# Two attention loops: three score banks in a ring, one bank for weighted sums, values products in halves

## What is computed

```python
x = _layernorm(x + _L0_attn_ref(x, ...))                      # recurrence and channel mix
x = _layernorm(x + _L0_xattn_ref(x, ctx_1024, mask, ...))     # attention 0
x = _layernorm(x + _L0_ffn_ref(x, ...))
x = _layernorm(x + _L1_attn_ref(x, ...))                      # linear recurrence
x = _layernorm(x + _L1_xattn_ref(ctx_1024, x, ...))           # attention 1
x = _layernorm(x + _L1_ffn_ref(x, ...))                       # 8 experts, 2 per position

def attention(x, ctx, ...):            # q from x (2048), k and v from ctx (1601 rows)
    scores = q @ k.T * scale           # per head, 2048 x 1601
    attn = softmax(scores)             # attention 0: masked keys at -inf
    return (attn @ v) @ Wo.T
```

## Time and profile before

| | |
|---|---|
| median of three runs | 2498.0 us |
| span of the profiled execution | 2495.9 us |
| PE busy | 1964.2 us (79% of the span) |
| DVE busy | 1159.1 us (46%) |
| ACT busy | 1035.0 us (41%) |
| mean granted TensorE clock | 0.917 of 2.4 GHz |
| narrow attention, first score product to last copy of weighted sums | 359.4 to 628.6 us |
| wide attention, the same | 1173.5 to 1959.5 us |

### The profile page before, as it was taken

The page is one execution under the profiler, slowest core; times in us unless marked ns, Lnnn a source line. Parts: engine busy times, 40 slices in busy tenths (PEclk is TensorE's granted clock), DMA queues, the critical chain, the costliest instruction groups (busy, mean ns, idle before and its releaser), DMA issues.

```text
span 2495.9 us, 27607 instructions
## 1 busy us (share of the span) xinstructions
PE 1964.2 (79%) x7552; PEld 794.0 (32%) x7553; DVE 1159.1 (46%) x1674; ACT 1035.0 (41%) x1606; POOL 221.1 (9%) x188
## 2 busy tenths in 40 slices
PE   5789869998798757628888888888887627999990
PEld 2334412222243223303222222222221225666660
DVE  4652367664211434438767667666660121111114
ACT  2332327666312343301666566666667501222220
POOL 1030100000201003200000000000000140000004
PEclk8899969999899879857999999999999958999995
DMA  7000130001000000370000000000000351000003
GB/s 252 0 0 0 33 94 25 25 21 53 1 0 4 0 0 27 69 127 7 8 7 14 8 8 7 8 15 8 7 1 1 140 207 33 28 26 28 27 26 103
DMA packets 63282, 90.41 MB, mean 36 GB/s; under 512 B 14144, under 2 KB 56320, under 8 KB 61514
## 3 DMA queue, kind: packets, MB, share of 16 engines
q1 hardware_dynamic: 60106, 80.77, 11.1%
q0 software_dynamic: 3072, 8.39, 1.1%
HBM read 61.53 MB, written 27.20 MB: 36 GB/s over the span
## 4 chain that ended last, share of the span: by engine, by line
PE 45%; issue 10%; ACT 9%; DVE 5%; POOL 2%; DMA 2%; ACTq 1%; SPq 1%; DVEq 0%; POOLq 0%
PE ps L1046 8%; PE ps L1652 8%; PE ps L512 8%; ACT arena L1119 7%; PE ps L1037 6%; PE ps L982 4%; PE ps L1667 4%; DVE arena L1149 2%; PE ps L1310 2%; DMA qparts<-arena 1%; PE ps L1076 1%; PE ps L440 1%; POOL arena L1766 1%; PE ps L1660 1%; PE ps L1065 1%
## 5 line engine op out<-in xcount | busy, mean ns | idle before, releaser
L1119 ACT ACTIVATE arena<-ps,arena 128x512 f32<-128x512 f32 x1088 | 668.0, 683 | 448.5 <-PE ps L1037 447.0
L1149 DVE TENSOR_REDUCE arena<-ps 128x1 f32<-128x832 f32 (+1 forms) x768 | 674.2, 908 | 213.5 <-PE ps L982 207.9
L1037 PE MATMUL ps<-arena 100*128 100x512 bf16 x1088 | 389.9, 389 | 119.4 <-ACT arena L1119 109.0
L512 PE MATMUL ps<-arena 128*128 x832 | 379.7, 616 | 83.0 <-DVE arena L1451 25.0
L982 PE MATMUL ps<-arena 97*128 97x416 bf16 (+1 forms) x1280 | 364.0, 367 | 90.8 <-DMA arena<-qparts 61.9
L1046 PE MATMUL ps<-arena 128*32 128x512 f32 x2160 | 289.3, 608 | 0.0
L1037 PEld LDWEIGHTS ps<-arena 100*128 100x128 bf16 x1088 | 93.9, 96 | 524.2 <-ACT arena L1119 443.2
L512 PEld LDWEIGHTS ps<-arena 128*128 128x128 f32 x832 | 162.7, 197 | 298.0 <-issue 298.0
L1652 PE MATMUL ps<-arena 128*128 x608 | 198.2, 469 | 29.4 <-ACT arena L1720 29.4
L982 PEld LDWEIGHTS ps<-arena 97*128 97x128 bf16 x1280 | 121.5, 99 | 246.9 <-DVE arena L1149 104.2
L1847 DVE TENSOR_TENSOR arena<-ps,arena 128x352 f32<-128x352 f32 x76 | 39.9, 525 | 272.5 <-ACT arena L1727 272.5
(11 more groups left out here) (186 smaller groups left out, 1403.7 us busy)
## 6 DMA issues: line engine op xcount, KB each, us to landing
arena<-in_experts_w SPq DMA_DIRECT2D x8, 2176.0 KB, 17.3
arena<-qparts SPq DMA_DIRECT2D x192, 64.0 KB, 2.3
qparts<-arena SPq DMA_DIRECT2D x24, 256.0 KB, 6.1
rows_in<-arena SPq DMA_DIRECT2D x1, 5120.0 KB, 31.8
arena<-kparts SPq DMA_DIRECT2D x12, 416.0 KB, 23.4
arena<-rows_in SPq DMA_DIRECT2D x38, 128.0 KB
rows_out<-arena SPq DMA_DIRECT2D x38, 128.0 KB, 1.7
arena<-in_w_rwkv SPq DMA_DIRECT2D x1, 2560.0 KB, 11.2
```

Of the source, the lines that this page charges most:

```text
L512: ins = eng.matmul(out, w[:, k, m * P:(m + 1) * P], x[:, k, tok(c)], start=k == 0, stop=k == ktiles - 1)
L1037: eng.matmul(score_bank(k), Kst[0:ROWS, g * HG + h, kt * P:(kt + 1) * P], Qst[0:ROWS, g, h, :], start=True, stop=True).then_inc(st_full.se ...
L1119: eng.activation(probs[:, keys_of(u, kt) % 2, h, :], score_bank(k), ACT.Exp, bias=zero_col).then_inc(p_full.sem, 1)
L1149: eng.tensor_reduce(MX[:, par, h * QT + q, e:e + 1], slot_banks(s_static)[:, 0:SIDE, 0:seg_keys], AX.XY, ALU.max).then_inc(slot_free.sem, 1)
```

## The change

All of it is in `attend` and what it calls.

1. **Ring of three score banks.** Banks 5, 6 and 7 take the scores in turn; score number k waits for the reader of number k-3. The denominators' product (`den`) no longer overwrites the old weighted sums but takes its own place in the ring.
2. **One bank for the weighted sums** (4). The first values product of a unit waits until the sums of the unit before are copied (`o_copied`). ScalarE makes this copy, no longer VectorE; it stands behind the fourth exponential of the next unit's first tile.
3. **Values products in halves.** Each is cut into two of 256 columns (`PV_CUTS`), placed at two points of the tile.
4. **New order in a tile**: score 0, item, score 1, score 2, first half of the values, item, score 3, second half, (third item). Wide: `den` stands between scores 1 and 2 of tile 2.
5. **First pass over 1602 keys** in the wide case: products over 401, 401, 400 and 400 keys (before: four of 416). In the narrow case an item is two heads, in the two banks of a slot, with one maximum that writes both, negated, in place; `negate` falls away there. 8 items per unit, two per tile.
6. The turn of the maxima waits for all maxima before it (`slot_free` up to s_count; before: s_count - 1).
7. Exponentials, logarithms and inversions take the bias as an immediate 0.0.

```diff
+            RING, RING_UNIT = 3, HG * n_kt + 1
+            PV_CUTS = 2
-            AT_DEN, AT_TURN, AT_INVERT, AT_OUT = (1, 1, 2, 3) if window else (2, 5, 4, 8)
+            AT_DEN, AT_TURN, AT_OUT = (1, 1, 3) if window else (2, 5, 8)
...
                 for kt in range(n_kt):
                     want = PAIRS * (kt + 1) // n_kt if first_pass else 0
-                    mid = (taken + want) // 2
+                    mine = list(range(taken, want)) + [None] * 3
+                    values = (kt - 1, 0) if kt else (n_kt - 1, -1)
                     yield ("scores", kt, 0)
-                    if kt == 0 and u > 0:
-                        yield ("pv", n_kt - 1, -1)
+                    if mine[0] is not None:
+                        yield ("item", mine[0])
                     yield ("scores", kt, 1)
-                    for pair in pairs[taken:mid]:
-                        yield ("pair",) + pair
+                    if kt == AT_DEN and u > 0 and not window:
+                        yield ("den",)
                     yield ("scores", kt, 2)
+                    if has_values:
+                        yield ("pv",) + values + (0,)
+                    if mine[1] is not None:
+                        yield ("item", mine[1])
                     yield ("scores", kt, 3)
...
+            def ring_bank(r):
+                return ps[:, 5 + r % RING, :]
+            def ring_wait(eng, u, i, r):
+                if r >= RING:
+                    ring_read.wait(eng, ring_before(i) + (r - RING + 1))
...
-            def score_bank(k):
-                return ps[:, 4 + k % 2, :]
-            def o_bank(u):
-                return ps[:, 6 + u % 2, :]
+            o_bank = ps[:, 4, :]
...
                 def turn_max(i_par, s_static, s_count):
-                    slot_free.wait(eng, s_count - 1)
+                    slot_free.wait(eng, s_count)
...
+                def values(w, kt, cut):
+                    at = cut * PVW
+                    for h in range(HG):
+                        ins = eng.matmul(o_bank[32 * h:32 * h + 32, at:at + PVW], Vaug[:, kt, (w % 4) * HG + h, :],
+                                         probs[:, keys_of(w, kt) % 2, h, at:at + PVW],
+                                         start=kt == 0 and cut == 0, stop=kt == n_kt - 1 and cut == PV_CUTS - 1,
...
+                            if kt == 0 and cut == 0 and u > 0:
+                                o_copied.wait(eng, i)
+                            values(u + before, kt, cut)
...
+                def copy_o(u, i):
+                    pv_done.wait(eng, n_kt * i)
+                    if u >= 3:
+                        o_norm.wait(eng, i - 2)
+                    eng.activation(Osb[:, (u - 1) % 2, :], o_bank, ACT.Copy).then_inc(o_copied.sem, 1)
...
-                            eng.activation(probs[:, keys_of(u, kt) % 2, h, :], score_bank(k), ACT.Exp,
-                                           bias=zero_col).then_inc(p_full.sem, 1)
+                            eng.activation(probs[:, keys_of(u, kt) % 2, h, :], ring_bank(r), ACT.Exp,
+                                           bias=0.0).then_inc(ring_read.sem, 1)
```

More of the change, by code:

```diff
@@ L870, in plan @@
                 first_pass = u <= 5
-                pairs = [(q, h, e) for q in range(QT) for h in range(HG) for e in range(ENDS)] if first_pass else []
                 taken = 0
@@ L895, in plan, with ring_place, ring_before, values_after @@
                         yield ("out", 1)
+            def ring_place(u, step):
+                return [s for s in plan(u) if s[0] in ("scores", "den")].index(step)
+            def ring_before(i):
+                return 0 if isinstance(i, int) and i == 0 else i * RING_UNIT - 1
+            def ring_bank(r):
[3 more added lines that the diff above has]
+                    ring_read.wait(eng, ring_before(i) + (r - RING + 1))
+                elif u > 0:
+                    lengths = {1: (RING_UNIT - 1, RING_UNIT)}.get(u, (RING_UNIT,))
+                    late = min((n - 1 - r) % RING for n in lengths)
+                    ring_read.wait(eng, ring_before(i) - late)
             BASE = 2 * PAIRS + 1
-            def values_after(i, q, h, e):
-                n = (q * HG + h) * ENDS + e
+            def values_after(i, n):
                 return range(n_kt * n // PAIRS, n_kt * (n + 1) // PAIRS) if i == 1 else ()
             def slots_before(u):
-                return BASE + sum(1 for v in range(u) for s in plan(v) if s[0] in ("pair", "turn_max", "out"))
+                return BASE + sum(1 for v in range(u) for s in plan(v) if s[0] in ("item", "turn_max", "out"))
             assert slots_before(5) - slots_before(1) == SLOTS
@@ new lines, in unit @@
+                            r = ring_place(u, step)
+                            ring_wait(eng, u, i, r)
+                            eng.matmul(ring_bank(r), Kst[0:ROWS, g * HG + h, kt * P:(kt + 1) * P],
+                                       Qst[0:ROWS, g, h, :], start=True, stop=True).then_inc(ring_full.sem, 1)
+                        elif what == "pv":
+                            _, kt, before, cut = step
+                            if before:
+                                ring_read.wait(eng, ring_before(i))
+                            else:
+                                ring_read.wait(eng, ring_before(i) + (ring_place(u, ("scores", kt, HG - 1)) + 1))
+                            if kt == 0 and cut == 0 and u > 0:
+                                o_copied.wait(eng, i)
+                            values(u + before, kt, cut)
+                        elif what == "item":
+                            _, n = step
@@ L1063, in unit @@
                         elif what == "den":
-                            o_copied.wait(eng, i)
-                            eng.matmul(o_bank(u - 1), pick_den, Osb[:, (u - 1) % 2, :], start=True,
-                                       stop=True).then_inc(den_out.sem, 1)
+                            denominators(u, i, ring_place(u, step))
                         elif what == "out":
@@ L1080, in _ @@
                 run_units(eng, unit)
-                p_full.wait(eng, 4 * n_kt * 16)
-                for h in range(HG):
-                    ins = eng.matmul(o_bank(15)[32 * h:32 * h + 32, :], Vaug[:, n_kt - 1, 3 * HG + h, :],
-                                     probs[:, keys_of(7, n_kt - 1) % 2, h, :], start=False, stop=True)
-                ins.then_inc(pv_done.sem, 1)
-                o_copied.wait(eng, 16)
-                eng.matmul(o_bank(15), pick_den, Osb[:, 1, :], start=True, stop=True).then_inc(den_out.sem, 1)
+                ring_read.wait(eng, ring_before(16))
+                for cut in range(PV_CUTS):
+                    values(7, n_kt - 1, cut)
+                denominators(8, 16, 0)
                 s = slots_before(8)
@@ L1111, in unit @@
                     i = unit_of(u, c)
+                    to_invert = None
                     for step in plan(u):
```

190 lines of the change are left out of this document (96 added, 94 removed).

## The result

Four runs of the changed kernel gave 2332.31 to 2334.47 us, median 2333.1, against 2498.08 for four runs of the kernel before: a ratio of 0.934, 95% interval 0.933 to 0.936. The forecast was 2334. The profiled span fell from 2495.9 to 2332.6 us, by 163.3.

What follows compares the result with a forecast made beforehand. TensorE was taken as the bound, losing time to mutual waits with ScalarE. Savings of 103 + 21 + 30 + 6 + 4 = 164 us from 2495.9 gave 2332, with 2.1 added 2334 us; range 2300 to 2400.

Steps and rivals of the forecast that it cites:

- The bound: Wide loops: TensorE, busy 536 of 608 us, is nearest to full; it and ScalarE each wait once per tile.
- The price of a half: Values product on TensorE: a half costs 0.66 us, 0.24 fixed plus 2 x 0.213; possible from 0.43 to 1.09.
- rival E: Values products: a half costs nearly a whole, 1.09 us, so the kernel gets slower, 2565 us; chance 0.06.
- Wide units with a first pass: Wide loops: a unit takes 41.0 us against 48.35, 7.3 saved in each of 14 units, 103 us.
- Rival D: Looped wide and narrow units: the denser TensorE stream runs out of instructions, +58 us, 2392 us; chance 0.08.
- The turn: Turn of the maxima in a wide unit: 0.11 us as before plus 0.45 for waiting for the item just ahead.
- Narrow units: Narrow loops: a unit with a first pass takes 13.7 us against 15.83, 30 us saved; last two units 6.
- First passes ahead of the loops: Stretches where VectorE sets the pace: 64 wide items x 0.03 us, about as much narrow, 4 us saved.
- B: Unit starts: the first values product waits for the copy of sums, 1.5 us in 32 units, 2382 us; chance 0.14.
- C: Each tile: one score wait of 0.28 us remains on TensorE, +67 us, 2401 us; chance 0.08.
- F: Whole change: nothing comes of it, TensorE's work fills what it gains at 0.9 us a half; chance 0.02.
- A: Whole kernel: the sum of savings holds, 2334 us, own range 2305 to 2365; chance 0.62.

## Why the prediction was right

- **The bound.** TensorE and ScalarE waited for each other, TensorE was the fuller one, and with the waits gone it is the bound: 88% busy before, 98% after. The run with two banks brings the waits back, and 110 us; the run over 1664 keys shows that more columns on TensorE are more time.
- **The price of a half** was 0.66 us, from rows 3 and 5: measured 0.66. This was the widest term, between 0.43 and 1.09, and the one on which rival E hung; the run with the halves together shows that the fixed part belongs to the visit to the 32-column form. Beside this price the prediction puts the time without a drain 65 us lower, 0.12 us for each of 544 halves. That is the price of doubling the visits; without any fixed part its own 0.24 a half would make 131.
- **Wide units with a first pass**: 41.0 us worked out, 41.25 measured; 14 units were to give 103. First to last copy and the first unit gave 118.2, the last two units 23.1 of it (21 expected), 95 for the others. Some 8 us are missing: 0.25 a unit, and the units with a Wo product, of which the three saved 6.3, 3.9 and 7.1 us instead of 7.3 (51.8, 53.8 and 48.1 us for 58.1, 57.7 and 55.2). Where the loop turns back TensorE stood for "issue": the first time 2.44 us, as before (2.42), the second time 3.16 us, where it had been 1.97. Timeline of PE after, and the busy times behind the second stop (columns as in the earlier trace rows), after and then before:

```profile
1518.24 0.60 PE L1080 MATMUL ps<-arena 100*128 100x512 bf16 x1 [3.16 <-issue]
```

```profile
1518.00:1524.00 6.00, 5.75 (x26) 1.52 (x27) 1.99 (x2) 2.61 (x5) 0.00 (x0) 0.50 0.19 53
...
1628.00:1634.00 6.00, 5.40 (x32) 1.64 (x31) 4.05 (x5) 4.95 (x8) 0.00 (x0) 1.00 0.12 31
```

 After this stop the granted clock was 0.50, the level of 1.2 GHz; before, it stayed at 1.00. The 5.75 us of work at that level would be some 2.9 at the full one (an estimate). With the 1.2 us by which the stop was longer that comes to 4.1 us, which covers the 3.4 us that the second of these units saved too little. The prediction had put the loop's turn as unchanged and had no term for the clock.

 Rival D would be this wait inside units as well; all "issue" ahead of scores is 8.5 us in the whole execution, at four places (the first score of each attention and the wide loop's two turns), so it fell.
- **The turn**: 0.45 us expected, 0.34 measured by taking it away. The terms that the prediction names (0.4 + 1.0 - 1.05) make 0.35, so it was the sum that was off.
- **Narrow units**: 13.7 worked out, 13.42 measured; 36 us expected with the last two, 39.1 measured between the copies.
- **First passes ahead of the loops**: the mis-sized term. 2 us wide came as worked out; narrow gave 6.7 us where about 2 was put (6.0 to 6.8 in the other kernels, which all have the double items: 25.2 to 26.0 us). Timeline of DVE after, narrow first pass of unit 1:

```profile
347.13 2.33 DVE L1204 TENSOR_REDUCE arena<-ps 128x2 f32<-128x1024 f32 x2
349.39 0.46 DVE L1236 TENSOR_SCALAR arena<-ps,arena 128x256 f32<-128x256 f32 x1
349.78 2.33 DVE L1204 TENSOR_REDUCE arena<-ps 128x2 f32<-128x1024 f32 x2
```

 Two items and one placing of values (L1236) take 2.65 us (347.13 to 349.78), with no idle time. Before, the same four heads and one placing took 4.12 us (347.90 to 352.02). Timeline of DVE before, a round's maxima and two placings (L1180):

```profile
347.90 2.68 DVE L1149 TENSOR_REDUCE arena<-ps 128x1 f32<-128x512 f32 x4
351.60 0.48 DVE L1180 TENSOR_SCALAR arena<-ps,arena 128x256 f32<-128x256 f32 x1 [1.02 <-PE ps L1000]
...
358.79 0.48 DVE L1180 TENSOR_SCALAR arena<-ps,arena 128x256 f32<-128x256 f32 x1 [0.16 <-PE ps L1000]
```

 VectorE waited 1.02 us for TensorE's product ahead of the placing, and I had counted only the maxima. Two things ended this wait. One is the granted clock: before, it was 0.50 (the level of 1.2 GHz) until 356.7 us, and the last of the four rounds, behind its rise, took 3.04 us with a wait of 0.16; after, it rose at 343.4. The other is the double items: in the run over 1664 keys a round at 0.50 took 3.20 us, with a wait of 0.37. The four rounds took 15.4 us before and 10.6 after, 4.8 less; the other 1.9 are in the first pass of unit 0. Why the clock rose earlier is not shown; it first rose at 341.8 to 348.0 us in all kernels with double items.
- **Sum**: 164 expected, 163.3 in the span. The misses cancel. Too much was put on the 14 wide units (8 us); too little on the narrow stretch (8 us: 39.1 + 6.7 for 36 + 2) and on the last two wide units (2 us). Stretches that the change does not touch took 2.7 us longer. The accuracy of 1 us is luck; the sum was good to some 8.
- **Rivals.** B (the single bank stalls) fell: the idle time ahead of all values products is 0.7 us. C fell: of the 9.2 us ahead of scores none ends with an exponential, and in a wide unit none is hidden either (the starts above). E and F fell with the price of a half. A remained.

The expectations of the experiments were worse than the prediction (58 and 50 us expected of whole or joined products, -10 and 32 measured), since they moved the values product by TensorE's prices and did not walk VectorE's two slots and the ring itself through the new order.

## What to carry to other kernels

When two engines each show idle time until the other, count the distance in the queue between a bank's writer and its next writer, and compare it with write, latency, read and release (here 1.24 us before, 1.07 with the shorter exponential in the run with whole products); one more bank is worth the wait times the number of tiles, and its price is another buffer's second bank. Split or move a long product only with every ring that runs through it in view: here the halves cost 0.22 us a tile for a second visit to the 32-column form and earned it back as distance, and the best version found keeps them together where items separate the scores and apart where nothing does. Shortening an operation of an engine off the path pays only in the stretches where it is the path (4 us of 90 here, with three banks). When a stretch changes more than its work explains, look at the granted clock there before giving the change the credit.

## What the runs showed of the hardware

- Entering and leaving the 32-column form costs TensorE 0.22 to 0.24 us a visit, whether 8 instructions of 512 columns or 16 of 256 stand in between (0.99 and 1.01 us from first to next). A full-width fp32 product between bf16 ones costs nothing beyond its columns (0.86 us).
- An activation of 128x512 from PSUM takes 598 ns with an immediate bias and 688 with one from SBUF; the next in a chain starts 0.49 or 0.58 us after it.
- A product can start late without any idle time in its row, while the engine still reads as busy from the product before; the wait then stands in the row of its weight load. In the run with the halves together this hid 0.25 us in the tile shown.
